# One core, two graph layers: the first layer's value products and probability transposes put next to each other, in the middle of the third projection

## The reference, cut to what matters

```python
h = jnp.einsum('bnd,ade->bane', feat_in, W)
th = jnp.tanh(h)
attn_src = jnp.einsum('bane,aeo->bano', th, w_src)
attn_dst = jnp.einsum('bane,aeo->bano', th, w_dst)
attn = attn_src + jnp.swapaxes(attn_dst, 2, 3)
attn = jnp.where(attn >= 0, attn, LEAKY_ALPHA * attn)
attn = jax.nn.softmax(jnp.where(mask, jnp.float32(-999.0), attn), axis=-1)
feat_out = jnp.einsum('banm,bame->bane', attn, h) + b
...
feat_out = jax.nn.elu(feat_out)
gate = jax.nn.sigmoid(feat_in @ H_w.T + H_b)
return gate * feat_out + (1.0 - gate) * feat_in
...
x = _layernorm(x + _L0_gnn_ref(...))
x = _layernorm(x + _L1_gnn_ref(...))      # q, k, v, softmax, ctx @ Wf
```

## Time and profile before

| | us |
|---|---|
| median of 3 runs (2763.75 to 2770.96) | 2765.53 |
| the profiled execution, its own time | 2766.33 |
| its span, first to last instruction | 2764.6 |
| busy: PE / DVE / ACT / POOL | 2726.9 / 1668.8 / 1160.3 / 1066.3 |

### The profile page before, as it was taken

How to read it: one execution, slowest core, us unless ns; L and a number is a source line. 1 busy time by engine, 2 the same in 40 slices (tenths; PEclk the granted TensorE clock), 3 DMA queues, 4 the chain that set the end, 5 groups by cost and what they waited for, 6 DMA issues and landing times.

```text
span 2764.6 us, 51821 instructions
## 1 busy us (share of the span) xinstructions
PE 2726.9 (99%) x20988; PEld 2517.8 (91%) x20988; DVE 1668.8 (60%) x3334; ACT 1160.3 (42%) x3045; POOL 1066.3 (39%) x630
## 2 busy tenths in 40 slices
PE   8999999999999989999999999999999999999998
PEld 6877778888788889999999999999999999999998
DVE  6888998888888754444454444454445445444443
ACT  5666776666666633322332233322332233223322
POOL 2453344433444134433444343434443343434340
PEclk9999999999999999999999999999999999999999
DMA  5656665555555512222213222222222222222220
GB/s 180 173 131 145 164 160 145 139 139 139 141 137 143 175 59 69 69 71 81 70 58 81 76 75 58 79 72 71 69 68 71 81 70 58 81 81 70 58 70 23
DMA packets 306894, 269.49 MB, mean 97 GB/s; under 512 B 227808, under 2 KB 244192, under 8 KB 306656
## 3 DMA queue, kind: packets, MB, share of 16 engines
q1 hardware_dynamic: 306656, 266.19, 35.5%
HBM read 142.65 MB, written 75.89 MB: 79 GB/s over the span
## 4 chain that ended last, share of the span: by engine, by line
PE 85%; DVE 5%; DMA 4%; issue 2%; POOL 2%; ACT 2%; SPq 1%; DVEq 0%; ACTq 0%; POOLq 0%
PE ps_hg L1036 21%; PE ps_a L1199 14%; PE ps_k L70 14%; PE ps_q L70 14%; PE ps_a L70 14%; PE ps_c L1165 2%; PE ps_s L1140 2%; PE ps_pv L1068 1%; DMA dst_all<-dst_scratch 1%; ACT logits L564 1%; PE ps_t L1055 1%; PE ps_pt L1165 1%; DMA dst_scratch<-dst 1%; PE ps_pt L1147 1%; DVE logits L770 1%
## 5 line engine op out<-in xcount | busy, mean ns | idle before, releaser
L1036 PE MATMUL ps_hg<-w_hi,xT 128*128 128x512 f32 x2268 | 745.6, 401 | 8.3 <-DVE h_one L803 8.2
L1036 PEld LDWEIGHTS ps_hg<-w_hi,xT 128*128 128x128 f32 x2268 | 426.1, 188 | 112.6 <-issue 11.3
L1036 PE MATMUL ps_hg<-w_lo,xT 128*128 128x512 f32 x1134 | 448.4, 395 | 0.0
L70 PE MATMUL ps_k<-x1T_hi,wk_hi 128*128 128x256 f32 x1152 | 329.1, 286 | 0.0
L70 PE MATMUL ps_q<-x1T_hi,wq_hi 128*128 128x256 f32 x1152 | 323.5, 281 | 1.4 <-DVE x1T_lo L910 1.4
L70 PE MATMUL ps_q<-x1T_lo,wq_hi 128*128 128x256 f32 x1152 | 322.6, 280 | 0.0
L70 PE MATMUL ps_k<-x1T_lo,wk_hi 128*128 128x256 f32 x1152 | 321.9, 279 | 0.0
L70 PE MATMUL ps_q<-x1T_hi,wq_lo 128*128 128x256 f32 x1152 | 321.9, 279 | 0.0
L70 PE MATMUL ps_k<-x1T_hi,wk_lo 128*128 128x256 f32 x1152 | 321.1, 279 | 0.0
L496 POOL TENSOR_TENSOR th_src<-th,wsrc_all 128x768 f32<-128x768 f32 x64 | 118.3, 1848 | 483.7 <-DVE dst_all L783 463.4
L648 ACT ACTIVATE qT<-ps_q,bq_col 128x256 f32<-128x256 f32 x192 | 80.5, 470 | 479.3 <-PE ps_q L70 479.3
(11 more groups left out here) (144 smaller groups left out, 5814.2 us busy)
## 6 DMA issues: line engine op xcount, KB each, us to landing
x_tok<-x SPq DMA_DIRECT2D x64, 384.0 KB, 4.1
dst_all<-dst_scratch SPq DMA_DIRECT2D x128, 192.0 KB, 3.4
gate_scratch<-gate SPq DMA_DIRECT2D x64, 384.0 KB, 2.6
feat_scratch<-feat SPq DMA_DIRECT2D x128, 192.0 KB, 2.8
feat_in<-feat_scratch SPq DMA_DIRECT2D x62, 384.0 KB, 3.1
gate_in<-gate_scratch SPq DMA_DIRECT2D x62, 384.0 KB, 3.7
x_even<-x SPq DMA_DIRECT2D x16, 768.0 KB, 4.2
x_odd<-x SPq DMA_DIRECT2D x16, 768.0 KB, 4.4
```

The lines of the kernel that those rows point to most:

```text
L70: ins = pe.matmul(out, left[a][c], right[b][c], start=(n == 0), stop=(n == len(terms) - 1))
L1036: ins = pe.matmul(ps_hg[:, cols], left[a][c], right[b][c], start=(c == 0 and n == 0), stop=(c == KC - 1 and n == 2))
```

## The change

TensorE: `project(2, T)` is cut into two halves of nine matmuls. The first half now comes before `values(T - 2)`, then `transpose_probs(T - 1)` follows at once, then the second half, which signals `g_done`. ScalarE: `copy_probs(T - 1)` follows `exp_scores(T - 1)` in the same iteration, ahead of `elu_exp(T - 2)`, where it stood at the start of the next iteration. VectorE: `bias_h(T)` comes before `attention(T - 2)`.

```diff
@@ scalar, the loop over T
-                if T >= 2:
-                    copy_probs(T - 2)
+                if T == 2:
+                    copy_probs(0)
...
                 exp_scores(T - 1)
                 if T >= 2:
+                    copy_probs(T - 1)
                     elu_exp(T - 2)
@@ scalar, after the loop
             round_x1(0)
-            copy_probs(NT - 2)
             leaky_scores(NT - 1)
@@ vector
                 if T >= 2:
+                    bias_h(T)
                     attention(T - 2)
-                    bias_h(T)
@@ tensor
-            def project(k, T):
+            def project(k, T, chunks=range(KC)):
...
-                for c in range(KC):
+                for c in chunks:
...
                 project(1, T).then_inc(h_done, 1)
+                project(2, T, range(KC // 2))
                 if T >= 2:
                     values(T - 2)
-                project(2, T).then_inc(g_done, 1)
-                if T >= 2:
                     transpose_probs(T - 1)
+                project(2, T, range(KC // 2, KC)).then_inc(g_done, 1)
```

## The result

The changed kernel takes 2776.60 us (median of 8 runs, 2773.23 to 2780.58), the kernel before 2767.65 (8 runs beside it, 2763.75 to 2771.22). The ratio is 1.0033, 95% interval 1.0021 to 1.0044: 9 us slower, outside the predicted range, whose upper end was 2773. The engines' orders changed as they were meant to. The loss came through a round trip of transfers whose own order the change left as it was.

What follows compares the result with a forecast made beforehand. TensorE, 99% busy, was taken as the bound; 0 - 1.4 + 0.7 + 1.1 = +0.4 us on the profiled 2766.33 gave 2766.7, or 2765.9 as median of runs. The range was 2758 to 2773.

Steps and rivals of the forecast that it cites:

- TensorE's own sequence: TensorE, small blocks in each tile: new neighbours and order neither add nor save, 0 us, bounds 10.5 gain to 7.4 loss.
- The rival on the laid-bare load: TensorE, transposes behind value products: first weight load can't run ahead, 7.4 us or more lost, 2773 to 2780; chance 0.07.
- The rival on the small blocks: TensorE, value products next to transposes: the exit bubble goes, 10.5 us less, 2755; chance 0.08.
- The waits: TensorE in layer 0's late tiles: exp limit moves from V + 2.61 to V + 2.81, seven runs gain 0.20 each, 1.4 us.
- one of the prediction's own signs of being wrong: Layer 0's tiles: forecast is wrong if stalls appear in tiles that had none, or the steady period moves over 0.1 us.
- cover for the elu's delay: VectorE's queue: idle times of 0.68 ahead of `rest_x` and 1.08 ahead of L770 hide the elu coming 1.07 us later.
- The steady tile's 1.16 of margin: Steady tile: exp ends at V + 1.65, TensorE waits only after V + 2.81, V being the value products' old start.
- ScalarE's order: ScalarE's copies ahead of the elu: free in steady tiles, three tiles between 165 and 245 us lose 0.7 us.
- The end of layer 0: After the last tile: copies ahead of the elu's steps delay layer 1's first transposes, a loss of 1.1 us.
- The exp is late in ordinary tiles: Layer 0's loop: elu's 1.07 us delay reaches the scores through `rest_x`; 5 us, or 2778 to 2784 if most tiles; chance 0.06.
- The waits go entirely: Layer 0's loop: later elu store gives the spread of `dst` room, late exps come earlier, up to 8.8 us, 2757; chance 0.04.
- the bounds of TensorE's edges: TensorE, edges of the small blocks: from 10.5 us gained by a vanished exit bubble to 7.4 lost by an exposed load.

Runs made afterwards that it cites:

- the load moved: Changed kernel with SyncE's load of a later `x_tok` tile issued behind the store of `dst` instead of ahead: 2768.28 us against 2766.21, ratio 1.0007.
- two padded kernels: Changed kernel with ten value products per tile issued twice, plus 0 or 128 TensorE instructions once at the first tile: 2784.57 and 2796.41 us against 2766.68.

## Why the prediction was wrong, by its steps

**TensorE's own sequence, 0 (bounds -10.5 to +7.4).** Right: the loads follow at 0.86 as worked out from the earlier trace rows, and the period went from 14.313 to 14.27, -2.4 us in all, nearer to 0 than to either bound. The rival on the laid-bare load did not occur. The rival on the small blocks did, at a quarter of its size: 0.04 per tile instead of 0.17, and only where the two blocks are neighbours. "Neither add nor save" was that much off.

**The waits, -1.4.** This step failed: "The same late tiles stall, each run of them by 0.20 less". Time lost was 19.0 instead of 8.8 - 1.4 = 7.4, and in the late part of the loop most of it lies in tiles that had waited for nothing before: one of the prediction's own signs of being wrong. I held the moment at which the exp ends fixed and moved only the threshold. But that moment comes out of a loop over `dst`, with a lap near 14.1 us beside TensorE's 14.3, of which the store's time is a term, and nothing in the sum asked what the change does to that store. The earlier trace rows held the sign: the idle time ahead of L770 "waits for ScalarE's scores", which wait for the spread `dst`. I listed it as cover for the elu's delay, and did not ask what sets it. The steady tile's 1.16 of margin was that of tiles whose store is short.

**ScalarE's order, +0.7.** Not separable at this size; with the old order the loop lost no less (21.0 against 19.0). The cover in a steady tile held, as the step said: with the load moved, the 45 late periods with this order lose nothing.

**The end of layer 0, +1.1.** Right in size: 1.06. Its reason, the copies ahead of the elu, is borne out for half: with ScalarE's old order 0.5 came back, and the other half was not found.

**The rivals.** "The exp is late in ordinary tiles" (0.06) named what happened, PE's waits for L598, 21 of them, and its price was 2778 to 2784 for most tiles and 5 us for some; measured are 9. But its mechanism, the elu's delay through `rest_x`, was wrong: ScalarE's old order would have cured it and did not. "The waits go entirely" had the right object with the wrong sign: it gave the spread of `dst` more room, and its transfer got slower. What it held against itself, that most late tiles of the kernel before carry extra work, was right. The sum's terms missed 10 us because the loop with the second longest lap was not priced, and the range was set from the bounds of TensorE's edges, which were not the uncertain term.

**What stays open.** That the value products' move brings the packets to the store is shown by the counts of the experiments, not why a packet starts where it does within TensorE's stream. Why the same move costs 4.0 us of lost time in the kernel before and 9.3 with the other parts in place was not tested, nor what makes layer 1 of two padded kernels 4 to 5 us longer. The 1.6 us at the start of the kernel were not taken apart; part of it (25.62 to 26.60 at `project(0)` of the second tile, by the timelines) lies ahead of any moved instruction.

## What to carry to other kernels

Where one engine is 99% busy, still measure the lap of every other closed loop (transfers and in-order queues included) and compare it with the period: here a lap of 14.1 to 15.5 stood beside 14.3, and only the difference between them protects the bound. Read the chain over the stretch in question, not the shares alone, and take a near tie as a width in the range. Where such a loop binds, keep a small transfer that lies in it ahead of large loads on its queue (some 7 us here in the changed kernel, nothing in the kernel before, where it did not bind), and look at what an engine with thousands of tiny instructions brings with it on the DMA engines.

## What the runs showed of the hardware that I had not expected

Instruction packets of 16 KB, 0.4% of the DMA engines' time, lengthen a 6 KB store beside them: 2.1 to 3.3 us between neighbours of one kernel. Of the stores shown, the one alone took 1.4, those beside a 384 KB load 2.1 and 2.4, those with both 3.3 and 3.8; with the packet but without the load ahead it was 2.1 on average (14 stores). With the same work per tile, the packets' place moved this loop by some 5 us of 900. TensorE changes from quarter-array products to whole-array transposes at no visible cost: their loads follow 0.86 us after the products' first, as the scores' of layer 1 do, and the tile is 0.04 us shorter than with the two apart.
